# Cross-attention over 16 batches: the low halves of the probabilities transposed by one DMA for two heads, the high halves as float16 on PE, and the value products three heads behind

## The reference, cut to what matters

```python
q   = heads(x @ W_q)                       # B=16, S=112, C=320, H=20 heads of 16
k_t = heads(text @ W_k); v_t = heads(text @ W_v)          # text: 371 tokens of E=512
probs_t  = softmax(q @ k_t.T * Dh**-0.5)                  # 112 x 371 for each head
text_out = probs_t @ v_t
k_ip, v_ip = heads(ip @ W_k_ip), heads(ip @ W_v_ip)       # ip: the last 4 tokens
qsem  = l2norm(probs_t @ text)                            # 112 x 512 for each head
sem   = qsem @ l2norm(ip).T
probs_ip = softmax(q @ k_ip.T * Dh**-0.5 + 0.5 * sem) * mask
out = (text_out + probs_ip @ v_ip) @ W_out + b_out + x
```

## Time and profile before

| | |
|---|---|
| median of 3 runs | 786.95 us (786.87 to 787.3) |
| the profiled execution | 787.76 us, of which the span of the engines is 786.0 us |
| busy share of the span | PE 96%, DVE 84%, ACT 74%, POOL 57% |
| mean granted clock of PE | 0.984 of full speed |

### The profile page before, as it was taken

One profiled execution on the slowest core, in us unless ns is written; L12 is line 12 of the kernel. 1 busy time (PEld: TensorE's weight loads), 2 busy tenths in 40 slices (PEclk: granted clock), 3 DMA queues, 4 the chain that ended last, 5 costly groups with the idle time before them and its releaser, 6 DMA issues.

```text
span 786.0 us, 23801 instructions
## 1 busy us (share of the span) xinstructions
PE 752.7 (96%) x7730; PEld 589.2 (75%) x7730; DVE 661.3 (84%) x1960; ACT 583.6 (74%) x1702; POOL 445.5 (57%) x558
## 2 busy tenths in 40 slices
PE   5899999999999999999999999999999999999983
PEld 3568778787877878787787878778787777878661
DVE  4878898988989898898989889898998989889883
ACT  4378787877878787787878778787877878777770
POOL 4035574656647465664746566474656647464762
PEclk8999999999999999999999999999999999999996
DMA  8313222221412223140222314022231402021000
GB/s 268 100 50 74 73 68 61 61 79 43 104 27 67 63 58 81 42 107 24 68 65 57 83 41 107 21 70 65 54 87 38 109 22 69 19 52 42 9 2 15
DMA packets 71465, 50.02 MB, mean 64 GB/s; under 512 B 16640, under 2 KB 71280, under 8 KB 71344
## 3 DMA queue, kind: packets, MB, share of 16 engines
q1 hardware_dynamic: 67648, 44.66, 21.9%
q10 hardware_dynamic: 3696, 3.84, 1.7%
HBM read 20.80 MB, written 2.38 MB: 29 GB/s over the span
## 4 chain that ended last, share of the span: by engine, by line
PE 91%; issue 2%; DVE 2%; POOL 2%; DMA 1%; ACT 1%; ACTq 0%; SPq 0%; POOLq 0%; DVEq 0%
PE ps_prep L475 22%; PE ps_gram L574 19%; PE ps_pT L556 13%; PE ps_gram L575 12%; PE ps_score L548 6%; PE ps_prep L530 5%; PE ps_val L582 2%; PE ps_val L584 2%; PE ps_prep L527 1%; PE ps_prep L505 1%; PE ps_prep L610 1%; PE ps_prep L507 1%; DMA xt_sb<-in_x_t 1%; POOL dual L407 1%; POOL nrm L417 1%
## 5 line engine op out<-in xcount | busy, mean ns | idle before, releaser
L407 POOL TENSOR_TENSOR dual<-prob 112x371 f32<-112x371 f32 x320 | 282.9, 884 | 302.4 <-ACT prob L753 283.2
L574 PE MATMUL ps_gram<-gram_hi,pT_hi 125*128 125x371 f16 (+1 forms) x960 | 303.9, 320 | 0.0
L575 PE MATMUL ps_gram<-gram_lo,pT_hi 125*128 125x371 f16 (+2 forms) x960 | 255.9, 267 | 0.0
L747 ACT ACTIVATE pT_hi<-ps_pT 125x336 f16<-125x336 f32 x320 | 144.6, 452 | 143.4 <-PE ps_pT L556 139.9
L737 ACT ACTIVATE prob<-ps_score,low 112x371 f32<-112x371 f32 x320 | 184.0, 575 | 16.3 <-DVE low L912 9.8
L912 DVE TENSOR_REDUCE low<-ps_score 112x1 f32<-112x371 f32 x320 | 171.3, 535 | 28.5 <-PE ps_score L548 24.8
L917 DVE TENSOR_TENSOR pT_lo<-ps_pT,pT_hi 125x336 f16<-125x336 f32 x320 | 160.0, 500 | 38.2 <-ACT pT_hi L747 34.0
L927 DVE CUSTOM_DVE_ANT_0 quad_junk<-ps_gram,dual 112x371 f32<-112x371 f32 x320 | 171.1, 535 | 12.4 <-PE ps_gram L575 6.0
L753 ACT ACTIVATE prob<-prob 112x371 f16<-112x371 f32 x320 | 168.9, 528 | 0.0
L582 PE MATMUL ps_val<-val,pT_hi 125*128 125x42 f16 (+1 forms) x960 | 166.8, 182 | 0.0
L556 PE MATMUL ps_pT<-ident,prob 112*125 112x112 f32 x960 | 156.9, 272 | 5.6 <-DVE pT_lo L917 3.7
(11 more groups left out here) (183 smaller groups left out, 1405.8 us busy)
## 6 DMA issues: line engine op xcount, KB each, us to landing
ctx_sb<-in_ctx_t SPq DMA_DIRECT2D x15, 750.0 KB, 4.5
k_st<-k_lo SPq DMA_DIRECT2D x62, 70.3 KB, 2.1
k_st<-k_hi SPq DMA_DIRECT2D x60, 70.3 KB, 2.1
q_st<-q_hi SPq DMA_DIRECT2D x64, 48.0 KB, 2.0
k_st<-k_lo SPq DMA_DIRECT2D x62, 46.9 KB, 2.0
q_st<-q_lo SPq DMA_DIRECT2D x60, 48.0 KB, 2.0
k_st<-k_hi SPq DMA_DIRECT2D x60, 46.9 KB, 2.0
x_sb<-in_x SPq DMA_DIRECT2D x16, 140.0 KB, 2.4
```

What stands on the lines that cost most here:

```text
L407: nc.gpsimd.tensor_tensor(dual[:, h % 2, :], prob[:, h % 4, 0:TX], prob_16[:, h % 2, :], ALU.subtract).then_inc(s_dual, 1)
L574: nc.tensor.matmul(ps_gram[h % 2][:, 0:TX], hi, gh[0:TROWS[i], i, :], start=(i == 0), stop=False, skip_group_check=True)
L575: last = nc.tensor.matmul(ps_gram[h % 2][:, i * TC:TX], hi, gl[0:TROWS[i], i, i * TC:TX], start=False, stop=(i == NT - 1), skip_group_chec ...
```

## The change

The low and the high half of the probabilities are now split before the transpose, not after it. ACT copies the probabilities to float16 (`prob_hi`, new `probs_hi`, in the place of `halve`, two heads ahead). POOL subtracts that from the probabilities and writes the float16 low half (`prob_lo`, new `probs_lo`), for two heads side by side. PE transposes `prob_hi` as float16, and ACT copies the result to `pT_hi` (`turned_out`). The low halves of two heads are transposed by one DMA (`turn_lo`, 112 rows of 768 float16) from SP into `pT_lo`. The value products, which need the low half, follow three steps behind the Gram products (`VAL_LATER`). `dual` is now twice the probabilities minus the high half, and DVE computes it (`duals`, in the place of its `probs_lo`).

Beside this: text rows are cut at 128 and not at 125; the low halves of all five pieces for the batch after next go to POOL; q and k are written to DRAM in two DMAs each and read back stacked in four each, in the place of 16 each from SBUF to SBUF; the first half of each batch's norms and inverse roots is computed within the batch (before, in the last batch alone); the copies of the image values to `vip_diag` are spread over the first steps.

```diff
-TC = T // 3
+TC = P
-POOL_PIECES = (2, 3, PIECE_X)
+POOL_PIECES = (0, 1, 2, 3, PIECE_X)
+HI_SLOTS = 4
+PT_HI_SLOTS, LO_PAIRS, PT_LO_PAIRS = 8, 2, 4
+VAL_LATER = 3
...
+            def turn_lo(b, h):
+
+                pair = (H * b.n + h) // 2
+                sp.wait_ge(s_prob_lo, 2 * pair + 2)
+                reached(sp, s_val, 2 * (pair + 1 - PT_LO_PAIRS))
+                sp.dma_start_transpose(pT_lo[:, pair % PT_LO_PAIRS, :, 0:S],
+                                       prob_lo[:, pair % LO_PAIRS, :, :].rearrange("s a t -> s (a t)")).then_inc(s_pT_lo[pair % PT_LO_PAIRS], 16)
...
             def body(b, prepare, turning, finishing):
...
+                for h in range(H):
+                    if h % 2 and h + 1 < H:
+                        turn_lo(b, h + 1)
+                    elif h % 2 and prepare:
+                        turn_lo(b.next(), 0)
...
+            def probs_lo(b, h):
                 g = H * b.n + h
+                pool.wait_ge(s_prob_hi, g + 1)
+                freed = g // 2 - LO_PAIRS
+                reached(pool, s_pT_lo[freed % PT_LO_PAIRS], 16 * (freed // PT_LO_PAIRS + 1))
+                nc.gpsimd.tensor_tensor(prob_lo[:, g // 2 % LO_PAIRS, g % 2, 0:TX], prob[:, h % 4, 0:TX], prob_hi[:, h % HI_SLOTS, 0:TX],
+                                        ALU.subtract).then_inc(s_prob_lo, 1)
...
             def transposes(b, h):
                 g = H * b.n + h
-                pe.wait_ge(s_prob, g + 1)
-                reached(pe, s_pT_lo, g)
+                turned = ps_pT[:, :].bitcast(F16)[:, 0:NT * S]
+                pe.wait_ge(s_prob_hi, g + 1)
+                reached(pe, s_pT_hi, g)
                 for i in range(NT):
-                    last = nc.tensor.transpose(ps_pT[0:TC, i * S:(i + 1) * S], prob[:, h % 4, i * TC:(i + 1) * TC],
-                                               ident[0:S, 0:S])
+                    last = nc.tensor.transpose(turned[:, i * S:(i + 1) * S], prob_hi[:, h % HI_SLOTS, i * TC:(i + 1) * TC],
+                                               ident_16[0:S, 0:S])
...
+            def turned_out(b, h):
+                g = H * b.n + h
+                act.wait_ge(s_pT, g + 1)
+                reached(act, s_val, g + 1 - PT_HI_SLOTS)
...
-                    if h + 1 < H:
-                        halve(b, h + 1)
+                    if h + 2 < H:
+                        probs_hi(b, h + 2)
```

More of the change, by code:

```diff
@@ L378, in batch_k_ip @@
             def batch_k_ip(a):
[L380 removed]
+                reached(pool, s_kst[1 - a.odd], stacked(a.last()) if a.n else 0)
                 for k_, ip in ((k_hi, kip_hi), (k_lo, kip_lo)):
@@ L461, in tail @@
                 for step in range(TEXT_OUT_STEP + 1):
-                    end(b.last(), step, ahead=True)
+                    end(b.last(), step)
             all_batches(body, tail)
@@ L565, in products @@
                     pe.wait_ge(s_prep_lo, NM * (b.n + 1))
-                pe.wait_ge(s_pT_lo, g + 1)
+                pe.wait_ge(s_pT_hi, g + 1)
                 reached(pe, s_quad, g - 1)
[L568 to L584, removed]
-                                            stop=(i == NT - 1), skip_group_check=True)
-                    if i == NT - 1:
-                        last.then_inc(s_val, 1)
@@ L596, in products, with late_values @@
                     for i in range(NT):
-                        gram_part(i)
-                        val_part(i)
+                        val_part(*late, i)
+                        if i + 1 < NT:
+                            gram_part(b, h, i + 1)
+            def late_values(b, h):
+                values_ready(b, h)
+                for i in range(NT):
+                    val_part(b, h, i)
             def finish(f, k, made):
@@ L675, in tail @@
             def tail(b):
+                for h in range(H - VAL_LATER, H):
+                    late_values(b.last(), h)
                 for k in range(NF):
@@ L705, in make_hi @@
                     if j == 0:
-                        reached(act, s_kst[1 - a.odd], 256 * (a.last().pair + 1))
+                        reached(act, s_kst[1 - a.odd], stacked(a.last()) if a.n else 0)
                     m = channels(j)
@@ L709, in make_hi @@
                 elif k == PIECE_Q:
-                    reached(act, s_qst[1 - a.odd], 256 * (a.last().pair + 1))
+                    reached(act, s_qst[1 - a.odd], stacked(a.last()) if a.n else 0)
                     for e in range(2):
@@ L840, in tail @@
             def tail(b):
+                half_out(b.last(), 1)
                 fin_exp(b.last())
@@ L880, in make_lo @@
                 elif k == PIECE_Q:
-                    reached(dve, s_qst[1 - a.odd], 256 * (a.last().pair + 1))
+                    reached(dve, s_qst[1 - a.odd], stacked(a.last()) if a.n else 0)
                     for e in range(2):
@@ L1107, in body @@
                         split_lo(b.next().next(), SPLIT_STEP[h])
-                    if not prepare and h in AHEAD_NORM_STEPS:
-                        norms_ahead(b, AHEAD_NORM_STEPS.index(h))
+                    for k in range(SOFT_NORMS):
+                        if h == AHEAD_NORM_STEPS[k]:
+                            norms_ahead(b, k)
             def tail(b):
                 for k in range(SOFT):
-                    soft(b.last(), k, ahead=True)
+                    soft(b.last(), k)
                 for k in range(NF):
```

248 lines of the change are left out of this document (162 added, 86 removed).

## The result

| | before | after |
|---|---|---|
| median of four runs | 786.97 us | 879.97 us (877.49 to 881.74) |
| ratio | | 1.118, 95% interval 1.115 to 1.121 |
| span of the profiled execution | 786.0 us | 877.5 us |
| busy share PE, DVE, ACT, POOL | 96, 84, 74, 57% | 84, 85, 68, 56% |
| mean granted clock of PE | 0.984 | 0.978 |

The account below looks back on a forecast made before the run. PE was taken to bound the kernel, busy 45.89 of 45.96 us a batch. Added were 27.7 over 15 batches, 1.7 and 0.5 at the end, 29.9 on 787.76; forecast 817 us, range 772 to 850.

Parts of the forecast that it names:

- PE's part: Three float16 transposes take 0.32 us to the end; each PE step 0.17 shorter, PE alone 42.1 us a batch.
- The ring: PE's transposes and ACT's step wait for each other: turn 1.88 or 2.28 us, batch 47.8, 27.7 us in all.
- 0.14 or 0.15 from a result to PE's start: Wait in us from ACT's prob_hi to PE's transposes, part of the 0.50 that closes a turn.
- DVE, POOL, SP: The other engines' work, with dual on DVE and text halves on POOL, fits in the 47.8 us batch.
- DVE stays at 40 of 47.8: DVE's busy us in a batch, if dual takes near 0.51, the lower end of 0.51 to 0.88.
- Long DVE rows for `dual`, with ACT waiting for the minimum: Sign in the new profile that the forecast is wrong: DVE's dual is slow and holds up ACT; no size given.
- behind a transpose that waits for POOL stand the loads and copies of the next batch; they have steps to spare: On SP's queue: DMA transposes delay the next batch's loads and copies at no cost.
- Last batch and ends: Last batch 1.7 us longer from twenty turns of 1.88, value products of the last three heads 0.5 more.
- (1): Rival: ACT reads float16 from PSUM much faster, so its turn is shorter than PE's step; 779 us, chance 0.18.
- (2): Rival: about the same time, with 0.42 for the 0.50 us that closes a turn; 787 us, chance 0.06.
- (3): Rival: DMA transposes land too late, about 8 us, and PE waits for its values; 883 us, chance 0.10.
- (4): Rival: PE's float16 transposes take as long as fp32 ones, a turn 0.16 longer; 868 us, chance 0.04.

Follow-up runs that it names:

- e7_pool_short: Changed kernel with early text load and prob_hi ahead of the exponentials, plus POOL's subtraction for prob_lo over 8 of 371 columns: 755.6 us.
- e5_ring_alone: Changed kernel with the early text load and dual computed for 64 of 371 columns, ACT's order unchanged: 806.9 us.
- e1: Changed kernel with the load of the next text issued in step 14 of the batch ahead, not in step 0 behind a DMA transpose: 852.4 us.
- e3: Changed kernel with prob_hi ahead of the exponentials on ACT and the text load in step 14: 803.6 us.
- e4_dual_short: Changed kernel with dual computed for 64 of 371 columns only, all else unchanged: 837.4 us, one run.
- e6_no_transpose: Changed kernel with the early text load and a plain DMA of 112x64 float16 in place of each DMA transpose: 851.2 us.

## Why the prediction was right or wrong

**The profile of before, PE's part: right for the transposes.** Three float16 transposes take 0.31 to 0.32 and what follows mostly starts 0.15 or 0.16 after them. PE is busy 44.88 of 52.19, more than the 42.1 of the forecast; the same instructions count 738.2 us in after and 703.6 in e7_pool_short, where a batch has 42.93 of 44.26, so most of the difference comes with the gaps. PE does not set the pace, as the forecast said.

**The ring: right in kind, priced 0.09 too high.** From `prob_hi`'s end to ACT's copy it is 0.41, not 0.50: the step that failed is "0.14 or 0.15 from a result to PE's start", a row between other engines; from ACT it is 0.05. A turn is 1.79 and 2.19, not 1.88 and 2.28. In steps 0, 14 and 18 PE's own work counts, so that alone makes the sum about 16 x 17 x 0.09 = 24 us less, 793. e5_ring_alone measured 806.9; of the 14 us between, ACT's 18 us of waits for the minimum, still there, may be the cause, which no run shows.

**"DVE, POOL, SP": wrong, and here is what is missing.** Two of its steps failed; the sum has both at nothing.

First, "DVE stays at 40 of 47.8": it is busy for 45.74 of 52.19. `dual` was taken near the lower end, 0.51. Alone it is 0.53, but more than half of the rows begin beside a POOL instruction and take 0.80; the mean is 0.68, the middle of the bounds, which makes 218 us of the 160 that the subtraction before took. The small operations of the second softmax, 53 us more, are in no term. The step behind it failed too, "add waits of a microsecond or two a batch": e1 against e5 puts DVE's part at 45.5 us, 3 us a batch. "Long DVE rows for `dual`, with ACT waiting for the minimum" stood among the signs of being wrong; they came, and had no price. A late minimum delays the exponentials, these delay `prob_hi`, and PE's transposes wait for that. So the ring and DVE are not two separate sums: taking out the ring's exponentials (e1 to e3, 49 us) or most of `dual` (e1 to e5, 45 us) each brings back most of the loss of 65 that e1 has.

The Trainium skill, in "SBUF — State Buffer", section "Who interferes with whom", says that a DVE instruction with two inputs in SBUF contends with a GpSimd instruction that reads SBUF, over ports that are an exclusive lock. The trace agrees: a stretched `dual` ends about 0.40 after POOL's instruction, and the sums with one input in PSUM show nothing; only beside POOL's powers, which read SBUF too, `dual` keeps its 0.54. The prediction read other pages and missed this rule, which spoke against moving `dual` to DVE while POOL keeps a subtraction a head. The timeline of the kernel before had shown it as well, a small DVE operation that starts beside POOL's `dual` and ends 0.14 after it (15 of its 16 rows begin beside `dual` and take 0.59 on the mean, the other takes 0.30):

```profile
388.36 0.84 POOL L407 TENSOR_TENSOR dual<-prob 112x371 f32<-112x371 f32 x1 [1.02 <-ACT prob L753]
388.74 0.60 DVE L988 SCALAR_TENSOR_TENSOR fprob<-fexp,mask_sb,fmax 112x80 f32<-112x80 f32 x1
```

Second, "behind a transpose that waits for POOL stand the loads and copies of the next batch; they have steps to spare". The copies have; the text has not. Its load is issued two steps before ACT wants it, and e1_ctx_early puts the price at 27.6 us.

Together: 806.9 for e5_ring_alone, 45.5 for DVE and 27.6 for the load make 880, but only because the last two are the differences on the way from after to e5_ring_alone. What tests them is the other way round, by e4_dual_short: 42.6 for DVE and then 30.5 for the load.

**Last batch and ends: the number right, in part by luck.** From the start of the last batch to the end it is 57.9 in the place of 55.9, 1.9 more against 2.2. But the turns of 1.79 would take 1.8 off the twenty of 1.88; longer steps, one of 3.36 among them, put it back.

**The rivals.** (1) fell: ACT's copy of the float16 bank takes 0.45 as that of the fp32 one did. Of (2) the condition came true, with 0.41 for its 0.42, and the time did not: its 787 counts twenty shorter turns in a batch where three are PE's, and like every rival it has neither DVE nor the load in it. The sign is the forecast's, the price of the ring alone lies nearer to (2). (3) gave nearly the measured number, 883, by a mechanism that does not occur: a transpose lands in 2.6 us, under the 3.7 that was taken, and e6_no_transpose gains 1 us. A number that fits is no evidence for its mechanism. The Trainium skill's 1309 ns a block, in "VectorE: DVE Perf Modes", section "The three transpose paths", would have made it an estimated 7.9 for the six blocks; the trace does not agree, and its 2.6 decides. (4) fell.

## What to carry to other kernels

When a copy is moved ahead of a transpose, look at where it stands in its engine's step: put what another engine waits for first and the rest behind it; here the exchange of two blocks was worth 49 us. In such a ring the lateness of other engines was not taken up again (27.6 us for a load, some 45 for DVE), so price the small waits behind it (a load's place in its queue, an operation that moves to a busier engine), and do not put them into the range. Before an operation with two SBUF operands goes to DVE, look at what POOL does at that time, and at the small operations whose place beside POOL shifts with it.

## What the runs showed of the hardware

The DMA transpose of 112x768 float16, 172 KB, landed in 2.6 us at the median (7.7 at most), between the plain DMAs of such a size in the same trace: 2.3 for 192 KB of `q_bounce`, 3.5 for 160 KB of `q_st`. SP was held for 1.2 us by its issue, for 0.5 by theirs. And the exclusion of DVE and POOL shows at small sizes as well: a `dual` of 64 columns begun beside POOL takes 0.53 on the mean, 0.21 without, and an operation of 80 columns 1.30 in the place of 0.24. POOL's powers are the exception: of the 35 rows of `dual` that began beside one in e3_both none takes more than 0.56.
